# Attention probabilities split before they are turned: float16 high halves by TensorE, low halves by DMA, values two heads later

## What is computed

```python
scores_t = einsum('bhsd,bhtd->bhst', q, k_t) * attn_scale
probs_t = softmax(scores_t)
text_out = einsum('bhst,bhtd->bhsd', probs_t, v_t)
attn_scores = einsum('bhsd,bhnd->bhsn', q, k_ip) * attn_scale
qsem = l2norm(einsum('bhst,bte->bhse', probs_t, text_ehs))
sem = einsum('bhse,bne->bhsn', qsem, l2norm(ip_ehs))
probs_ip = softmax(attn_scores + 0.5 * sem) * spatial_mask
ip_out = einsum('bhsn,bhnd->bhsd', probs_ip, v_ip)
out = (text_out + ip_out) @ W_out + b_out + residual
```

## Time and profile before

| | us |
|---|---|
| median of three runs | 787.72 |
| the profiled execution | 787.76 |
| its span, first to last instruction | 786.0 |
| TensorE busy | 752.7 |
| VectorE busy | 661.3 |
| ScalarE busy | 583.6 |
| GpSimd busy | 445.5 |

### The profile page before, as it was taken

The page is one execution under the profiler, slowest core; times in us unless marked ns, Lnnn a source line. Parts: engine busy times, 40 slices in busy tenths (PEclk is TensorE's granted clock), DMA queues, the critical chain, the costliest instruction groups (busy, mean ns, idle before and its releaser), DMA issues.

```text
span 786.0 us, 23801 instructions
## 1 busy us (share of the span) xinstructions
PE 752.7 (96%) x7730; PEld 589.2 (75%) x7730; DVE 661.3 (84%) x1960; ACT 583.6 (74%) x1702; POOL 445.5 (57%) x558
## 2 busy tenths in 40 slices
PE   5899999999999999999999999999999999999983
PEld 3568778787877878787787878778787777878661
DVE  4878898988989898898989889898998989889883
ACT  4378787877878787787878778787877878777770
POOL 4035574656647465664746566474656647464762
PEclk8999999999999999999999999999999999999996
DMA  8313222221412223140222314022231402021000
GB/s 268 100 50 74 73 68 61 61 79 43 104 27 67 63 58 81 42 107 24 68 65 57 83 41 107 21 70 65 54 87 38 109 22 69 19 52 42 9 2 15
DMA packets 71465, 50.02 MB, mean 64 GB/s; under 512 B 16640, under 2 KB 71280, under 8 KB 71344
## 3 DMA queue, kind: packets, MB, share of 16 engines
q1 hardware_dynamic: 67648, 44.66, 21.9%
q10 hardware_dynamic: 3696, 3.84, 1.7%
HBM read 20.80 MB, written 2.38 MB: 29 GB/s over the span
## 4 chain that ended last, share of the span: by engine, by line
PE 91%; issue 2%; DVE 2%; POOL 2%; DMA 1%; ACT 1%; ACTq 0%; SPq 0%; POOLq 0%; DVEq 0%
PE ps_prep L475 22%; PE ps_gram L574 19%; PE ps_pT L556 13%; PE ps_gram L575 12%; PE ps_score L548 6%; PE ps_prep L530 5%; PE ps_val L582 2%; PE ps_val L584 2%; PE ps_prep L527 1%; PE ps_prep L505 1%; PE ps_prep L610 1%; PE ps_prep L507 1%; DMA xt_sb<-in_x_t 1%; POOL dual L407 1%; POOL nrm L417 1%
## 5 line engine op out<-in xcount | busy, mean ns | idle before, releaser
L407 POOL TENSOR_TENSOR dual<-prob 112x371 f32<-112x371 f32 x320 | 282.9, 884 | 302.4 <-ACT prob L753 283.2
L574 PE MATMUL ps_gram<-gram_hi,pT_hi 125*128 125x371 f16 (+1 forms) x960 | 303.9, 320 | 0.0
L575 PE MATMUL ps_gram<-gram_lo,pT_hi 125*128 125x371 f16 (+2 forms) x960 | 255.9, 267 | 0.0
L747 ACT ACTIVATE pT_hi<-ps_pT 125x336 f16<-125x336 f32 x320 | 144.6, 452 | 143.4 <-PE ps_pT L556 139.9
L737 ACT ACTIVATE prob<-ps_score,low 112x371 f32<-112x371 f32 x320 | 184.0, 575 | 16.3 <-DVE low L912 9.8
L912 DVE TENSOR_REDUCE low<-ps_score 112x1 f32<-112x371 f32 x320 | 171.3, 535 | 28.5 <-PE ps_score L548 24.8
L917 DVE TENSOR_TENSOR pT_lo<-ps_pT,pT_hi 125x336 f16<-125x336 f32 x320 | 160.0, 500 | 38.2 <-ACT pT_hi L747 34.0
L927 DVE CUSTOM_DVE_ANT_0 quad_junk<-ps_gram,dual 112x371 f32<-112x371 f32 x320 | 171.1, 535 | 12.4 <-PE ps_gram L575 6.0
L753 ACT ACTIVATE prob<-prob 112x371 f16<-112x371 f32 x320 | 168.9, 528 | 0.0
L582 PE MATMUL ps_val<-val,pT_hi 125*128 125x42 f16 (+1 forms) x960 | 166.8, 182 | 0.0
L556 PE MATMUL ps_pT<-ident,prob 112*125 112x112 f32 x960 | 156.9, 272 | 5.6 <-DVE pT_lo L917 3.7
(11 more groups left out here) (183 smaller groups left out, 1405.8 us busy)
## 6 DMA issues: line engine op xcount, KB each, us to landing
ctx_sb<-in_ctx_t SPq DMA_DIRECT2D x15, 750.0 KB, 4.5
k_st<-k_lo SPq DMA_DIRECT2D x62, 70.3 KB, 2.1
k_st<-k_hi SPq DMA_DIRECT2D x60, 70.3 KB, 2.1
q_st<-q_hi SPq DMA_DIRECT2D x64, 48.0 KB, 2.0
k_st<-k_lo SPq DMA_DIRECT2D x62, 46.9 KB, 2.0
q_st<-q_lo SPq DMA_DIRECT2D x60, 48.0 KB, 2.0
k_st<-k_hi SPq DMA_DIRECT2D x60, 46.9 KB, 2.0
x_sb<-in_x SPq DMA_DIRECT2D x16, 140.0 KB, 2.4
```

Of the source, the lines that this page charges most:

```text
L407: nc.gpsimd.tensor_tensor(dual[:, h % 2, :], prob[:, h % 4, 0:TX], prob_16[:, h % 2, :], ALU.subtract).then_inc(s_dual, 1)
L574: nc.tensor.matmul(ps_gram[h % 2][:, 0:TX], hi, gh[0:TROWS[i], i, :], start=(i == 0), stop=False, skip_group_check=True)
L575: last = nc.tensor.matmul(ps_gram[h % 2][:, i * TC:TX], hi, gl[0:TROWS[i], i, i * TC:TX], start=False, stop=(i == NT - 1), skip_group_chec ...
```

## The change

- Tiles have 128 rows (`TC = P`): 128, 128 and 115.
- ScalarE no longer halves p. `probs_hi(h+2)` writes `prob_hi`, p in float16, not turned, at the end of step h, behind `exps(h+3)`.
- TensorE transposes `prob_hi` in float16 to a PSUM bank seen as float16, and ScalarE copies it out (`turned_out(h+1)`, at the start of the step).
- VectorE makes the low half before it is turned: `probs_lo(h+2)` is `prob` minus `prob_hi`, from SBUF, in the place where `probs_lo(h+1)` stood.
- SP turns the low half by one transposing DMA a head (`turn_lo(h+2)`), first in each of its steps. Between them the restack is spread, two DMAs a step, over the steps 2 to 9 (queries) and 8 to 15 (keys).
- The values of a head are made in the step two later (`VAL_LATER`), between the parts of that step's Gram product, and so is `half_out`. Before them TensorE waits for the DMA of the low half (`values_ready`).
- GpSimd's `dual` is p plus its low half (twice the old value, and the factor in the norm is halved).
- High and low halves have four slots each, turned and not turned.
- The norms of the first ten heads are taken ahead in every batch, in steps 14 to 17, with their inverse roots in steps 18 and 19; the steps of `soft` begin at step 3 instead of 2.

```diff
-TC = T // 3
+TC = P
...
-VALS_STEP, POW_STEPS, EXP_STEP = 0, (3, 4, 5, 6), 9
-
-SOFT_AT = {(2, 0): 0, (2, 1): 1, (2, 2): 2, (3, 0): 3,
+HI_SLOTS = LO_SLOTS = 4
+VAL_LATER = 2
+AHEAD_VALS_STEP, AHEAD_NORM_STEPS, AHEAD_POW_STEPS = 13, (14, 15, 16, 17), (18, 19)
+VALS_STEP, POW_STEPS, EXP_STEP = 2, (5, 6), 9
+
+SOFT_AT = {(3, 1): 0, (3, 2): 1, (4, 0): 2, (4, 1): 3,
            (7, 2): 4, (8, 0): 5, (8, 1): 6, (8, 2): 7, (9, 0): 8, (9, 1): 9,
            (10, 1): 10, (10, 2): 11, (11, 0): 12}
...
+            def turn_lo(b, h):
+
+                g = H * b.n + h
+                sp.wait_ge(s_prob_lo, g + 1)
+                reached(sp, s_val, g + 1 - LO_SLOTS)
+                sp.dma_start_transpose(pT_lo[:, h % LO_SLOTS, :, 0:S], prob_lo[:, h % LO_SLOTS, :]).then_inc(s_pT_lo[h % LO_SLOTS], 16)
...
+                for h in range(H):
+                    if h + 2 < H:
+                        turn_lo(b, h + 2)
+                    elif prepare:
+                        turn_lo(b.next(), h + 2 - H)
+                    if turning and h == 0:
+                        load_ctx(b.next().next())
+                        load_xt(b.next().next())
...
+                    if prepare and 0 <= h - Q_STACK_STEP < 8:
+                        stack_q(b.next(), part=slice(2 * (h - Q_STACK_STEP), 2 * (h - Q_STACK_STEP) + 2))
+                    if prepare and 0 <= h - K_STACK_STEP < 8:
+                        stack_k(b.next(), part=slice(2 * (h - K_STACK_STEP), 2 * (h - K_STACK_STEP) + 2))
+                    if prepare and h == LOAD_X_STEP:
+                        load_x(b.next())
...
@@ -402,9 +436,9 @@
 
             def duals(b, h):
                 g = H * b.n + h
-                pool.wait_ge(s_prob_16, g + 1)
+                pool.wait_ge(s_prob_lo, g + 1)
                 reached(pool, s_quad, g - 1)
...
-            def end(f, step, ahead=False):
-                if step == VALS_STEP:
+            def end_ahead(f, step):
+                if step == AHEAD_VALS_STEP:
                     reached(pool, s_text_out, f.n)
                     reached(pool, s_soft, SOFT * (f.n - 1) + SOFT_ARGS)
-                    if not ahead:
-                        sum_values(f, 0)
+                    sum_values(f, 0).then_inc(s_ahead, 1)
+                if step in AHEAD_POW_STEPS:
+                    pool.wait_ge(s_ahead, AHEAD * (f.n + 1))
+                    inverse_roots(AHEAD_POW_STEPS.index(step))
+
...
 
             def transposes(b, h):
                 g = H * b.n + h
-                pe.wait_ge(s_prob, g + 1)
-                reached(pe, s_pT_lo, g)
+                turned = ps_pT[:, :].bitcast(F16)[:, 0:NT * S]
+                pe.wait_ge(s_prob_hi, g + 1)
+                reached(pe, s_pT_hi, g)
                 for i in range(NT):
-                    last = nc.tensor.transpose(ps_pT[0:TC, i * S:(i + 1) * S], prob[:, h % 4, i * TC:(i + 1) * TC],
-                                               ident[0:S, 0:S])
+                    last = nc.tensor.transpose(turned[:, i * S:(i + 1) * S], prob_hi[:, h % HI_SLOTS, i * TC:(i + 1) * TC],
+                                               ident_16[0:S, 0:S])
                 last.then_inc(s_pT, 1)
...
+            def val_part(b, h, i):
+                r, o, v = TROWS[i], h % HH * 2 * VW, val[b.odd]
+                nc.tensor.matmul(ps_val[:, o:o + 2 * VW], pT_hi[0:r, h % HI_SLOTS, i, :], v[0:r, i, h, :], start=(i == 0), stop=False,
...
+            def values_ready(b, h):
+                g = H * b.n + h
+                pe.wait_ge(s_pT_lo[h % LO_SLOTS], 16 * (g // LO_SLOTS + 1))
+                if h % HH == 0:
+                    reached(pe, s_half, 2 * b.n + h // HH)
...
             def products(b, h):
 
@@ -563,39 +620,30 @@
                 g = H * b.n + h
                 if h == 0:
                     pe.wait_ge(s_prep_lo, NM * (b.n + 1))
-                pe.wait_ge(s_pT_lo, g + 1)
+                pe.wait_ge(s_pT_hi, g + 1)
                 reached(pe, s_quad, g - 1)
...
+                late = (b, h - VAL_LATER) if h >= VAL_LATER else (b.last(), h - VAL_LATER + H)
+                if g < VAL_LATER:
                     for i in range(NT):
-                        gram_part(i)
-                    reached(pe, s_half, 2 * b.n + h // HH)
+                        gram_part(b, h, i)
+                elif late[1] % HH == 0:
                     for i in range(NT):
-                        val_part(i)
+                        gram_part(b, h, i)
+                    values_ready(*late)
+                    for i in range(NT):
+                        val_part(*late, i)
                 else:
+                    gram_part(b, h, 0)
+                    values_ready(*late)
                     for i in range(NT):
-                        gram_part(i)
-                        val_part(i)
+                        val_part(*late, i)
+                        if i + 1 < NT:
+                            gram_part(b, h, i + 1)
...
             def tail(b):
+                for h in range(H - VAL_LATER, H):
+                    late_values(b.last(), h)
                 for k in range(NF):
                     finish(b.last(), k, NM * B)
...
                 g = H * b.n + h
                 act.wait_ge(s_low, g + 1)
                 reached(act, s_dual, g - 3)
+                reached(act, s_prob_lo, g - 3)
                 nc.scalar.activation(prob[:, h % 4, 0:TX], ps_score[h % 2][0:S, 0:TX], ACT.Exp, bias=low[:, h % 4:h % 4 + 1],
                                      scale=-1.0).then_inc(s_prob, 1)
                 if h == 0:
                     reached(act, s_soft, SOFT * (b.n - 2) + SOFT_ARGS)
                 nc.scalar.activation(ip_score[b.odd][:, h, :], ps_score[h % 2][0:S, TX:T], ACT.Copy).then_inc(s_ip_score, 1)
...
+            def turned_out(b, h):
+                g = H * b.n + h
+                act.wait_ge(s_pT, g + 1)
+                reached(act, s_val, g + 1 - HI_SLOTS)
+                turned = ps_pT[:, :].bitcast(F16)[:, 0:NT * S]
+                nc.scalar.activation(pT_hi[:, h % HI_SLOTS, :, 0:S], turned.rearrange("p (c s) -> p c s", s=S), ACT.Copy).then_inc(s_pT_hi, 1)
+
             def probs_hi(b, h):
                 g = H * b.n + h
-                act.wait_ge(s_pT, g + 1)
-                reached(act, s_val, g - 1)
-                nc.scalar.activation(pT_hi[:, h % 2, :, 0:S], ps_pT[0:TC, 0:NT * S].rearrange("p (c s) -> p c s", s=S), ACT.Copy).then_inc(s_pT_hi, 1)
-
-            def halve(b, h):
-                g = H * b.n + h
                 act.wait_ge(s_prob, g + 1)
-                reached(act, s_dual, g - 1)
-                nc.scalar.activation(prob_16[:, h % 2, :], prob[:, h % 4, 0:TX], ACT.Copy, scale=0.5).then_inc(s_prob_16, 1)
+                reached(act, s_pT, g + 1 - HI_SLOTS)
+                reached(act, s_prob_lo, g + 1 - HI_SLOTS)
+                reached(act, s_dual, g + 1 - HI_SLOTS)
+                nc.scalar.activation(prob_hi[:, h % HI_SLOTS, 0:TX], prob[:, h % 4, 0:TX], ACT.Copy).then_inc(s_prob_hi, 1)
...
             def body(b, prepare, turning, finishing):
                 for h in range(H):
                     if h + 1 < H:
-                        probs_hi(b, h + 1)
+                        turned_out(b, h + 1)
                     elif prepare:
-                        probs_hi(b.next(), 0)
+                        turned_out(b.next(), 0)
                     if prepare and h in TAKE_STEP:
                         make_hi(b.next(), TAKE_STEP[h])
                     if turning and h in SPLIT_STEP:
@@ -826,18 +881,21 @@
                         exps(b, h + 3)
                     elif prepare:
                         exps(b.next(), h + 3 - H)
...
+                    if h + 2 < H:
+                        probs_hi(b, h + 2)
                     elif prepare:
-                        halve(b.next(), 0)
+                        probs_hi(b.next(), h + 2 - H)
+                    if h == HH - 1 + VAL_LATER:
+                        half_out(b, 0)
+                    if finishing and h == VAL_LATER - 1:
+                        half_out(b.last(), 1)
                     if finishing and h == EXP_STEP + (0 if prepare else SOFT_LATER):
                         fin_exp(b.last())
                     if finishing and h == H - 1:
                         store(b.last())
 
...
             def probs_lo(b, h):
                 g = H * b.n + h
-                dve.wait_ge(s_pT_hi, g + 1)
-                nc.vector.tensor_tensor(pT_lo[:, h % 2, :, 0:S], ps_pT[0:TC, 0:NT * S].rearrange("p (c s) -> p c s", s=S),
-                                        pT_hi[:, h % 2, :, 0:S], ALU.subtract).then_inc(s_pT_lo, 1)
+                dve.wait_ge(s_prob_hi, g + 1)
+                reached(dve, s_dual, g + 1 - LO_SLOTS)
+                reached(dve, s_pT_lo[h % LO_SLOTS], 16 * (g // LO_SLOTS))
+                nc.vector.tensor_tensor(prob_lo[:, h % LO_SLOTS, 0:TX], prob[:, h % 4, 0:TX], prob_hi[:, h % HI_SLOTS, 0:TX],
```

(6 more changed lines are left out.)

145 lines of the change are left out of this document (72 added, 73 removed).

## The result

The kernel after takes 1109.88 us (median of four, 1108.92 to 1114.04) where the kernel before, beside it, takes 787.48 (787.11 to 787.75): 1.4105 times as long, 95% interval 1.407 to 1.414. The forecast was 1058, its range 1025 to 1180, and the narrower range of its own mechanism 1030 to 1095. The profiled execution has a span of 1108.5 us.

What follows compares the result with a forecast made beforehand. Before, TensorE was taken as the bound; after, a circle of waits between VectorE and ScalarE. Setup, batch 0 (59.9), thirteen batches at 63.0 (819), batch 14 (62.1), the last batch and the tail made span 1056.6, forecast 1058 us, range 1025 to 1180.

Steps and rivals of the forecast that it cites:

- rival A: DMA path binds: a turn costs over 2.0 us of SP or the rings, giving 1360 or 1840 us; chance 0.11.
- Rival B: TensorE, with gaps each step, drops to a lower clock: up to 1400 us, or 1100 to 1200 in part; chance 0.07.
- the signs named beforehand: TensorE under 75% busy, waiting most for prob_hi; VectorE idle at prob_lo; exponential waiting in nearly every head; 63 us per batch.
- The 63 us for twenty heads: One batch of twenty heads in the changed kernel was forecast at 63.0 us, where 45.1 stood before.
- The bound before, and the gain on TensorE: TensorE bound at about 2.25 us a head; three float16 transposes take 0.15 to 0.18 us, gaining some 0.15 a head.
- The ring on VectorE: VectorE's low halves wait for ScalarE's high halves, queued behind an exponential needing VectorE's latest minimum: 2.56 us a head.
- The 330 us: VectorE's total idle time ahead of prob_lo, about 1.05 us ahead of each of 320.
- VectorE's other work: VectorE's work per batch besides the heads' three operations: 10.9 us, added to 51.2 for twenty heads.
- Restack 0.4 a batch, bounds 0 and 2.: Last key restack pair, issued in step 15 behind a turning DMA, delays the next batch's first score: 0.4 us a batch.
- SP has ... 2 us of loads.: SP's time per batch: 32 restack issues (20 us) and 2 us of loads, the rest free for turns.
- The turning DMA: SP's transpose of each head's low half, taken as hidden: over three steps to land, twenty turns fit under 2.0 us each.
- Rival C, 740 without the ring.: High halves finish before the minimum, so VectorE does not wait and TensorE binds at 42.1 us a batch: 740; chance 0.03.

Runs made afterwards that it cites:

- the second copy: Changed kernel with context loads and restack moved earlier, plus ScalarE computing the high halves twice, first into an unread buffer: 1183.5 us, 1.503.
- the best version: Changed kernel with high halves ahead of ScalarE's exponential, context loads earlier, two heads' low halves per turning DMA, three restack DMAs a step: 875.87 us, 1.113.

## Why the prediction was right, and where it was off

The direction, the engine that waits and the operation it waits at came out as forecast. The time, 1110, lies 15 us above the range of the mechanism itself, 1030 to 1095. It lies within 1025 to 1180 because the lower part of the rivals A and B was taken in; A did not happen and B only in part, so that much of the range's success is luck. Of the signs named beforehand, TensorE's busy share (72%), its largest wait (197.9 us, for `prob_hi`) and the idle time ahead of `prob_lo` held. The 63 us for twenty heads were 66.5, ScalarE waited for the minimum in 214 of 320 heads and not in nearly all, and the sign for B, a clock under 1.00 in the middle, appeared (0.92 in 525:570).

- **The bound before, and the gain on TensorE.** Right: 0.31 to 0.16 us a head, inside 0.15 to 0.18 for the new one, and it bought nothing.
- **The ring on VectorE.** Right to the hundredth: 1.64 us from minimum to low halves, and a median of 1.10 us of idleness ahead of the low halves. In 188 of 320 heads the idleness is within 0.02 of that; in 63 it is under 1.00, as where a softmax step stands behind the minimum, and in 62 over 1.20, where something else is late. Shown by the order changed on either engine (wait 367.7 to 117.0 or 79.2 us) and by the second copy (318 x 0.39 us). The 330 us that the prediction names for this wait do not follow from its own 1.10 and 0.9, which make 338; with both transfers moved it was 339.4.
- **VectorE's other work.** Not measured apart. With both transfers moved and TensorE relieved 1064.5 us are left against 1058. The 1058 hold some 6 us of restack lateness that this version no longer has, and the 1064.5 hold 9.4 us of waits for TensorE, so ring and other work together came out within 4 us.
- **"Restack 0.4 a batch, bounds 0 and 2."** The place was right and the size too small, though within its bounds: moving the restack alone is worth 22.0 us, 1.5 for each of the 15 batches that are prepared. At these 15 first scores VectorE stood 15.8 us, from 0.41 to 2.27. The 0.4 came true in three batches. That the turning issue takes 1.20 us where a plain issue's 0.6 was put does not explain the others, since it took 1.20 in the three as well. In the others the turn of step 15 began up to 1.4 us after its low half was ready, or a restack issue took 1.1 to 1.3 us, or the transfer landed late; why is open.
- **"SP has ... 2 us of loads."** This is the step that failed: they were counted as SP's time and not as something that others wait for, so the lateness stands in the sum at nothing. The load stands behind a wait for VectorE's low half, and ScalarE needs it ahead of an exponential: 21.2 us alone, and 23.6 together with the restack. This is the rule that each queue that a step is moved past must be asked who waits behind; it was applied to the restack and not to the context.
- **The turning DMA.** Right that it is hidden behind the ring (0.2 us of waiting), so rival A did not happen. But "twenty turns fit while one costs less than 2.0 us" was near its limit: with the issue at 1.20, the restack steps need 2.58 us of SP, and without the ring that binds. Of the pages weighed there, the Trainium skill, Advanced Engine Details and Errata, section X-Bar Transpose (TRN2), holds for the landing (2.3 against 2.1) and not for the issue; the Trainium skill, VectorE: DVE Perf Modes, section The three transpose paths, has 1309 ns for one block, which did not act as a rate: three blocks land in 2.3 us and six in 2.7.
- **Rival B, the clock.** Partly there. The mean is 0.923, and in stretches the granted clock is 0.50. It costs little while the ring is longer than TensorE's step. Where a piece of preparation coincides with it TensorE comes late: with both transfers moved this cost 26.6 us of VectorE's waits, of which less work on TensorE took away 17.2, and with them 21.8 us of the time. No run has the full clock throughout, so the clock's own price is not shown.
- **Rival C, 740 without the ring.** It would not have come out so, for two reasons that it lacked: SP's issues (115 to 132 us), and the low halves' second SBUF operand. Before, VectorE's low half took one operand from PSUM and lasted 0.49 to 0.51 us; the 109 beside `dual` alone averaged 0.50 us, as did the 49 with no GpSimd operation beside them.

What stays open: the best version stands 89 us above the kernel before, of which `dual` explains 34. The low halves still average 0.65 us there against 0.50 before, some 48 us of VectorE in all. Some 15 of these are the longer operation (0.55 us for 371 columns, 0.50 for 336), the other 33 stand beside GpSimd's other operations. TensorE waits 29.6 us for the turned low halves. Which of these the remaining 55 us are was not tried.

## What to carry over

Write down, for each in-order engine, what every waiting instruction waits for in the same step on the other engine: an operation that needs the result of a step placed behind another that needs this engine's own latest result makes a ring. Its length, summed from rows, gave 1058 us for the 1110 measured, where TensorE's busy time gave 740. Then do the same for the queue of SP, with who waits for each transfer that stands behind a wait. A move that frees the busiest engine pays only if both sums stay under that engine's step.

## What the runs showed of the hardware

- A transposing DMA issued by SP holds it for 1.20 us for 112x384 halves and for 1.23 us for 112x768, against 0.6 for a plain one; they land in 2.3 and 2.7 us.
- A VectorE subtraction of two SBUF operands (112x371) takes 0.55 us alone, up to 1.18 us beside one GpSimd addition that reads SBUF and up to 1.87 beside two GpSimd operations in a row. The low halves before, with one operand in PSUM (125x336), stayed at 0.50 us in the mean beside the same GpSimd work.
- Three float16 transposes of 112 columns and 112 rows take 0.16 us on TensorE at a granted clock of 1.00, float32 ones 0.31, from start to start.
- TensorE's granted clock can fall after the gap or inside it. With both transfers moved it was 1.00 while TensorE was 9% busy (551 to 552) and 0.52 and 0.50 when it was fully busy again (553 to 555). With the order on ScalarE changed it was 1.00 for the part of the hole up to 593, fell to 0.52 in 593:594 with TensorE still idle, and the first 6 us of work behind the hole ran at 0.50. Either way the work behind the gap pays.
